# Zero matmuls on TensorE in front of the short waits of the first layer

## The reference, cut to what matters

```python
scores = einsum('bnd,d->bn', x, score_w[0]) + score_b[0]
_, idx = top_k(scores, 10)                      # 10 tokens of each half
picked = take_along_axis(x, idx[:, :, None], axis=1)
q = picked @ Wq.T + bq;  k = ctx @ Wk.T + bk;  v = ctx @ Wv.T + bv    # 16 heads of 8
attn = softmax(q k^T / sqrt(8));  o = attn v
x = x.at[arange(B)[:, None], idx].set(o @ out_w.T + out_b)
```

## Time and profile before

| what | us |
|---|---|
| median of 3 runs | 543.25 |
| lowest and highest of them | 539.63, 547.52 |
| the profiled execution, its own time | 540.42 |
| its span in the trace | 538.5 |
| TensorE busy (share of the span) | 412.6 (77%) |
| VectorE busy | 354.9 (66%) |
| mean granted clock of TensorE | 0.784 |

### The profile page before, as it was taken

How to read it: one execution, slowest core, us unless ns; L and a number is a source line. 1 busy time by engine, 2 the same in 40 slices (tenths; PEclk the granted TensorE clock), 3 DMA queues, 4 the chain that set the end, 5 groups by cost and what they waited for, 6 DMA issues and landing times.

```text
span 538.5 us, 8140 instructions
## 1 busy us (share of the span) xinstructions
PE 412.6 (77%) x2775; PEld 206.4 (38%) x2775; DVE 354.9 (66%) x802; ACT 254.0 (47%) x513; POOL 241.6 (45%) x378
## 2 busy tenths in 40 slices
PE   6889678757788999998989772566665756778597
PEld 3546455424334344334243550222232223324536
DVE  2744754556999311447384469999989898778442
ACT  2314433324000666643426327899977783447431
POOL 4051224349000344533201315999978896336320
PEclk9868957978999999999699996555555555556699
DMA  9400000000000000000000002698876677113301
GB/s 262 156 1 1 4 1 1 0 0 1 2 0 1 1 1 2 1 1 1 0 1 2 1 2 39 132 144 140 162 131 117 117 123 153 27 34 67 71 0 40
DMA packets 88975, 26.10 MB, mean 48 GB/s; under 512 B 81061, under 2 KB 88167, under 8 KB 88935
## 3 DMA queue, kind: packets, MB, share of 16 engines
q1 hardware_dynamic: 88935, 25.58, 24.5%
HBM read 5.61 MB, written 0.52 MB: 11 GB/s over the span
## 4 chain that ended last, share of the span: by engine, by line
PE 43%; DVE 27%; POOL 18%; issue 5%; ACT 4%; DMA 1%; POOLq 0%; DVEq 0%; ACTq 0%
POOL k_stack L573 12%; DVE k_stack L2068 8%; PE ps L837 5%; PE ps L852 4%; PE ps L638 3%; POOL stats L564 3%; PE ps L739 3%; DVE stats L2148 3%; PE ps L749 2%; DVE xh L1639 2%; PE ps L915 2%; DVE st L1630 2%; PE ps L630 2%; POOL rstd L483 2%; PE ps L773 2%
## 5 line engine op out<-in xcount | busy, mean ns | idle before, releaser
L2148 DVE TENSOR_REDUCE stats<-ps 128x2 f32<-128x1024 f32 x64 | 77.6, 1213 | 2.4 <-PE ps L1293 2.0
L1595 ACT ACTIVATE e_buf<-ps,stats,sders 128x512 f32<-128x512 f32 x88 | 67.6, 773 | 18.4 <-POOL stats L564 18.4
L1313 PE MATMUL ps<-k_stack,q_stack 128*32 128x128 bf16 x512 | 38.3, 307 | 37.9 <-DVE k_stack L2161 37.9
L573 POOL TENSOR_SCALAR k_stack<-e_buf,stats 128x512 int16<-128x512 f32 x88 | 63.0, 728 | 2.1 <-DVE stats L2155 1.5
L1441 ACT ACTIVATE e_buf<-ps 128x1024 f32<-128x1024 f32 (+3 forms) x44 | 28.2, 710 | 58.5 <-PE ps L837 58.5
L481 POOL TENSOR_SCALAR rstd<-mv 128x4 f32<-128x4 f32 x18 | 4.4, 243 | 99.3 <-DVE mv L1633 99.3
L1313 PEld LDWEIGHTS ps<-k_stack,q_stack 128*32 128x32 bf16 x512 | 22.0, 129 | 68.8 <-DVE k_stack L2161 66.0
L430 POOL TENSOR_SCALAR_AFFINE_SELECT e_buf<-e_buf 128x256 f32<-128x256 f32 x44 | 17.8, 412 | 66.8 <-ACT e_buf L1441 66.2
L1293 PE MATMUL ps<-q_stack 32*128 32x512 bf16 x128 | 37.6, 588 | 12.4 <-ACT e_buf L1595 8.9
L2068 DVE TENSOR_REDUCE k_stack<-ps 128x4 f32<-128x1024 f32 (+3 forms) x32 | 44.9, 1483 | 2.6 <-PE ps L796 2.6
L837 PE MATMUL ps<-k_stack,q_stack 32*128 32x512 f32 (+3 forms) x256 | 34.7, 478 | 0.6 <-ACT e_buf L1441 0.4
(11 more groups left out here) (277 smaller groups left out, 892.9 us busy)
## 6 DMA issues: line engine op xcount, KB each, us to landing
wsq<-in_squares SPq DMA_DIRECT2D x3, 384.0 KB, 4.8
k_stack<-k_stack SPq DMA_TRANSPOSE x64, 3.1
spread<-in_spread SPq DMA_DIRECT2D x1, 896.0 KB, 6.7
x<-in_x SPq DMA_DIRECT2D x1, 512.0 KB, 4.4
l_w<-in_L_xattn_W_ff SPq DMA_DIRECT2D x2, 256.0 KB, 7.2
l_w<-in_L_xattn_fc_w SPq DMA_DIRECT2D x2, 256.0 KB, 7.8
l_w<-in_L_xattn_ff_w SPq DMA_DIRECT2D x1, 512.0 KB, 8.8
out<-x SPq DMA_DIRECT2D x2, 256.0 KB, 2.3
```

The source lines that it names most:

```text
L573: pool.tensor_scalar(t_rows[n % TURNING][:, j, :], e_ring[n % len(e_ring)][:, j, :], stats[:, 2, c:c + 1], 0.0, ALU.mult, ALU.add).then_in ...
L1313: mm = pe.matmul(ps[BAND * band:BAND * (band + 1), 7, qb * P:(qb + 1) * P], v_band[:, kb, b, V * band + v, :], t_keys[n % len(t_keys)][:, ...
L1595: act.activation(e_ring[n % len(e_ring)][:, j, :], ps[:, 2 * (n % 3) + j, :], ACT.Exp, bias=stats[:, 1, c:c + 1], scale=sders[:, 8:9], acc ...
L2148: dve.tensor_reduce(stats[:, 0, c:c + 2], ps[:, 2 * (n % 3):2 * (n % 3) + 2, :], AX, ALU.max, negate=True).then_inc(S("ints.nm"), 1)
```

## The change

A helper `keep_warm(bank, n, columns)` issues n matmuls of the identity with 512 columns of zeros into a bank that nobody reads. Ten calls are added to TensorE's list: 28 such matmuls in layer 0 and 3 before `single_head`. Most stand directly ahead of a wait for another engine. Two waits are added as well: one for `heads.base` (the zeros are written) and one for the first `L0.kept` (bank 2 has been read). Nothing is removed or moved. Bank 3, 2 or 0 takes the zeros, and no signal is attached to them.

```diff
+            def keep_warm(bank, n, columns):
+
+                for _ in range(n):
+                    pe.matmul(ps[:, bank, :], ident16[:, :], columns, start=True, stop=True)
...
+            zeros = k_stack[:, 8 * NT:8 * NT + N]
+            pe.wait_ge(S("heads.base"), 1)
+            keep_warm(3, 2, zeros)
             pe.wait_ge(S("L0.rank"), 1)
...
             mm.then_inc(S("L0.rankT"), 1)
+            keep_warm(3, 2, zeros)
             pe.wait_ge(S("L0.onehot"), 1)
...
+            pe.wait_ge(S("L0.kept"), 1)
+            keep_warm(2, 2, zeros)
             pe.wait_ge(S("L0.picked.sb"), 1)
...
             turn_picked(0)
+            keep_warm(2, 1, zeros)
             pe.wait_ge(S("L0.qblk"), 1)
...
             turn_picked(1)
+            keep_warm(2, 10, zeros)
             pe.wait_ge(S("L0.p"), 1)
...
             mm.then_inc(S("L0.t"), 1)
+            keep_warm(2, 2, zeros)
             pe.wait_ge(S("L0.pt"), 1)
...
+            keep_warm(2, 4, zeros)
             pe.wait_ge(S("L0.oT"), 1)
...
             mm.then_inc(S("L0.ao.mm"), 1)
+            keep_warm(2, 2, zeros)
             pe.wait_ge(S("L0.ao"), 1)
...
+                keep_warm(0, 3, zeros)
                 pe.wait_ge(S("L1.sa.v"), B)
                 single_head()
```

## The result

The changed kernel took 532.97 us (median of 4 runs, 532.05 to 537.70), the kernel before 541.44 (median of 4, the earlier three among them). The ratio is 0.9894, with a 95% interval of 0.9852 to 0.9936, thus 5.7 us by the ratio, and 3.5 to 8.0 by its interval. The ratio is an estimate of its own that leaves out executions in a slower state (here the one of 547.52), so it is not the quotient of the two medians, which would give 8.5 us. Run again later on another chip (the last pair of experiments) it was 0.9885 (0.9837 to 0.9933). That is less than 2%, and clear of no change.

A forecast was written before the change was run, and what follows sets the result against it. No engine bounds the whole; in layer 0 a chain of short steps through TensorE, VectorE and ScalarE does, partly at half clock. Savings of 5.94 less 0.2 give 5.7 us: 543.25 - 5.7 = 537.5 us, range 532 to 543.5.

The forecast's parts named there:

- The chain runs through TensorE in the half-clock stretches: Layer 0, 22 to 43 us: one short step is always waited for, so slow matmuls are paid in full.
- The put-back: L1225 in layer 0, ten rows of the array: 3.75 us at half clock becomes 1.88, saving 1.87.
- the first projections: First four records of L638, after the put-back: 3.39 us becomes 1.72 at full clock, saving 1.67.
- L1217: Layer 0's output projection, ahead of the put-back: 1.04 us becomes 0.6 at full clock, saving 0.45.
- L1210: Layer 0, four records with 160 columns after ScalarE's copy: 1.10 us becomes 0.68, saving 0.4.
- the scores L1199: Layer 0, eight records bound by weight loads: 1.36 us becomes 1.0, saving 0.35 (bounds 0.1 and 0.65).
- The zeros hide, at 0.2 us for all: All nine calls fit into TensorE's waits at full clock; 0.2 us charged together for roundings, bounds 0 and 0.9.
- the covers: The steps of other engines that TensorE waits for, behind which each call hides; if shorter, zeros would be late.
- 45.98 to 49.39, 1.2 us: Half-clock stretch with L661: three zeros close the 0.78 us wait before it, saving 1.2, bounds 0 and 1.6.
- Rival 1: Clock falls in L1181 or L1225 as before, L638 partly slow: gain 3 us, time 540; chance 0.22.
- Rival 2: Zeros do not hold the clock and stand in the way at half clock: 545 or 547 us; chance 0.12.
- The Trainium skill's rule on idle gaps: Long idle gaps between bursts send the clock to half; by it, closing gaps like these would give nothing.

The follow-up runs named there:

- the last pair of experiments: e9 and e10, both against the same 11 runs of the kernel before (538.96 us): 525.32 and 533.01 us.
- e7: Changed kernel with every call issuing twice as many zero matmuls: 539.47 us, ratio 1.0008 to the kernel before.
- e3: Changed kernel without the three zero matmuls ahead of single-head attention, one execution: 531.69 us.
- e1: Changed kernel with 10 rows of identity and zeros instead of 128 in the added matmuls: 550.88 us, ratio 1.0217 to the kernel before.
- e10: The changed kernel itself once more, on the same chip as e9: 533.01 us, ratio 0.9885 to the kernel before.
- e5: Changed kernel with zero matmuls also in the waits of layer 1's cross-attention: 530.44 us, ratio 0.9831 to the kernel before.
- e9: Changed kernel with e5's calls, more zeros in layer 1 and on to layer 2, without the three ahead of single-head attention: 525.32 us, ratio 0.9741 to before.
- e6: Changed kernel without the first three calls (six zero matmuls, ahead of ranks, one-hot columns and query projection), one execution: 534.00 us.
- e8: Changed kernel with only the ten zero matmuls in the wait for the softmax, all other calls left out, one execution: 538.47 us.

## Why the prediction was right

The direction and the mechanism came out, and the size within what these runs can tell: 5.7 us were worked out, and 5.7 by the ratio were measured. That the two agree to a tenth is luck, since the interval runs from 3.5 to 8.0. The absolute time of 537.5 was 4.5 too high: 532.97 lies below the forecast's own range (533.5 to 541.5), and inside the final one (532 to 543.5) by 1 us only. The three runs of before that were shown had a median of 543.25; over all later runs it lies at 538.7 to 541.4. Taking the profiled execution as the base, 534.7, would have been nearer to 532.97. Point by point:

- **The chain runs through TensorE in the half-clock stretches**: right. The put-back fell from 3.75 to 1.91 on the chain (predicted gain 1.87), the first projections from 3.39 to 1.96 (1.43; predicted 1.67), L1217 from 1.04 to about 0.55 (predicted 0.45), L1210 from 1.10 to 0.81 (0.29; predicted 0.4), the scores L1199 from 1.36 to 0.81 (0.55; predicted 0.35). Together 4.6 against 4.7.
- **The zeros hide, at 0.2 us for all**: right. In the changed profile no step behind a call starts more than 0.1 us after its releaser could let it go (the ranks, L1232 and L1241 are the late ones). The prediction wrote 4.7 us and 39.2 for the first score matmul, but its own terms give 4.74 less 0.2, thus 4.5. Measured from the common step of VectorE it is 4.4; the lead by the clock of the trace is 4.0 because that step came 0.44 later. That delay is no cost of the zeros. That the covers are nearly used up is what e7 shows.
- **45.98 to 49.39, 1.2 us**: the size was near (the lead grows by 1.6 there), and the reason was wrong. I gave it to the three zeros; e3 has the same without them. The clock was full before that stretch and stayed full, and why it did is open. So this term came out without its reason.
- **Rival 1, the clock holds only in part**: it happens in some executions, and cheaply. The fall near 22 us, which the kernel before has too, came back in three of five profiles with all zeros of layer 0, and goes with 0.6 to 0.9 us more (table below). The run with ones shows the fall behind the put-back that the rival described.
- **Rival 2, the zeros do not hold the clock**: not so for matmuls with 128 rows of zeros. The price of zeros that do not hold it was far too low. With ten rows the loss was 11.7 us by the ratio, because the returns I had taken for granted did not come. Behind the chance of 0.12 stood 545 or 547, a loss of 0.3 to 0.7%; e1 suggests 2%.
- **The Trainium skill's rule on idle gaps** (TensorE: Matmul & The Clock Gate, section "Why this matters for your kernels"), by which closing gaps like these would give nothing: it gave 1.1%. The kernel before fell at 22.09 though no gap ahead of that exceeded 0.45 us, and e1 fell to half clock and stayed there with TensorE busy for 30.72 of 30.72 us. For the falls in this kernel the trace disagrees with long idleness as the only cause.

The table gives, for the kernel before and for those with the ten zeros and all that follow them in layer 0, the way from VectorE's common step (18.16 and 18.60 in the result) to the first score matmul:

| run | common step | first score matmul | between, us | clock at 0.50 near 22 us |
|---|---|---|---|---|
| before | 18.16 | 43.89 | 25.73 | yes |
| changed | 18.60 | 39.90 | 21.30 | no |
| e3 | 18.50 | 39.90 | 21.40 | no |
| e10 | 18.38 | 40.41 | 22.03 | yes |
| e5 | 17.96 | 40.07 | 22.11 | yes |
| e9 | 18.24 | 40.29 | 22.05 | yes |
| e6 | 18.19 | 40.40 | 22.21 | yes |

e6 lacks the first three calls, and e3 and e9 have none ahead of single-head attention. What all six share, and the kernel before does not, is full clock from 26 us at the latest through the put-back and the projections. With that alone they are 3.5 to 3.7 us shorter, and 4.3 to 4.4 where the fall near 22 stayed away as well.

## What to carry to other kernels

Where a chain of short steps runs through TensorE, read the granted clock by stretches and look at what the chain's matmuls cost at either clock: a handful of wide fp32 matmuls behind a chain of few-row ones can be worth more than everything in between. Full-row matmuls put into the waits helped to hold the clock here, if not in every execution. Each belongs in a wait that the trace shows and that is longer than it; in the doubled run the extra ones cost three quarters of their length. Filling only a part of the waits can be worse than filling none, as one execution showed. Compare such changes by many runs, and one profile only up to the edited place: where the later falls lie differs between executions by as much as the gain.

## What the hardware showed that was not expected

- TensorE busy without a pause, its added matmuls and its put-back on ten of 128 rows, was granted 0.50 for 30.72 us, the last 5.5 of them dense projections (e1); with 128 rows of zeros in the same places it was granted 1.00 for 51.20 us in one profile. So matmuls whose moving side is all zeros can take part in holding the clock.
- Sixteen matmuls with only ten moving columns, 1.95 us at full clock, took 3.59 at half (e1, e8): a gather with next to nothing to stream nearly doubles too.
- The same kernel's clock changed at different places in two executions: full from 12.74 to 63.94 in one; 0.50 from 22.57 to 25.98, 56.70 to 60.12 and from 63.53 on in the other.
